# Two projections split or stacked, row sums moved, and transpositions joined, in a fused recurrent and FP4 feed-forward kernel on TensorE

## What is computed

```python
s = attn(xn)                       # causal convolution, min-GRU, feed-forward with gelu
h = silu(fp4(xn) @ fp4(w_gate).T) * (fp4(xn) @ fp4(w_up).T)     # 704 hidden columns
g = silu(fp4(h) @ fp4(w_down).T)
out = x + s * g
```

## Time and profile before

| | |
|---|---|
| median of 3 runs | 1085.59 us (1084.41 to 1086.84) |
| the profiled execution | 1085.26 us |
| its span, first to last instruction | 1083.5 us |
| mean granted clock of TensorE in it | 0.997 of 2.4 GHz |
| busy share of TensorE, VectorE, ScalarE, GpSimd | 98%, 86%, 56%, 14% |
| from chunk to chunk in the middle | 63.98 us |

### The profile page before, as it was taken

One profiled execution on the slowest core, in us unless ns is written; L12 is line 12 of the kernel. 1 busy time (PEld: TensorE's weight loads), 2 busy tenths in 40 slices (PEclk: granted clock), 3 DMA queues, 4 the chain that ended last, 5 costly groups with the idle time before them and its releaser, 6 DMA issues. The chain is left out here.

```text
span 1083.5 us, 18319 instructions
## 1 busy us (share of the span) xinstructions
PE 1061.8 (98%) x6954; PEld 967.9 (89%) x6954; DVE 934.5 (86%) x1720; ACT 607.3 (56%) x967; POOL 147.5 (14%) x123
## 2 busy tenths in 40 slices
PE   7899999999999999999999999999999999999998
PEld 6788989989898998989999898998989899898998
DVE  6978988989888898988889898898989889898895
ACT  5564464564746547474654747455574645647452
POOL 1230101112020110201111010111101011120010
PEclk9999999999999999999999999999999999999999
DMA  7000001010010101001010010101001010100110
GB/s 248 1 21 1 1 2 59 1 60 1 1 59 1 59 1 47 13 2 59 1 60 1 21 40 1 59 1 60 1 1 59 1 59 1 59 1 2 39 40 21
DMA packets 29365, 31.45 MB, mean 29 GB/s; under 512 B 1120, under 2 KB 28512, under 8 KB 29280
## 3 DMA queue, kind: packets, MB, share of 16 engines
q1 hardware_dynamic: 28448, 29.43, 8.7%
q10 hardware_dynamic: 832, 0.87, 0.2%
HBM read 21.90 MB, written 8.39 MB: 28 GB/s over the span
## 5 line engine op out<-in xcount | busy, mean ns | idle before, releaser
L990 PE MATMUL gu_ps<-gu_hi,xq_hi 128*128 128x352 f32 x512 | 168.3, 329 | 0.0
L990 PE MATMUL gu_ps<-gu_lo,xq_hi 128*128 128x352 f32 x512 | 165.9, 324 | 0.0
L990 PE MATMUL gu_ps<-gu_hi,xq_lo 128*128 128x352 f32 x512 | 165.7, 324 | 0.0
L990 PE MATMUL w_ps<-w_hi,act_hi 128*128 128x256 f32 x480 | 140.1, 292 | 0.0
L990 PE MATMUL w_ps<-w_hi,act_lo 128*128 128x256 f32 x480 | 135.1, 281 | 0.0
L990 PE MATMUL w_ps<-w_lo,act_hi 128*128 128x256 f32 x480 | 134.9, 281 | 0.0
L990 PE MATMUL w_ps<-dn_hi,hqt_hi 128*128 128x256 f32 x384 | 116.6, 304 | 2.0 <-DVE hqt_lo L519 2.0
L990 PE MATMUL w_ps<-dn_hi,hqt_lo 128*128 128x256 f32 x384 | 108.5, 283 | 0.0
L990 PE MATMUL w_ps<-dn_lo,hqt_hi 128*128 128x256 f32 x384 | 108.4, 282 | 0.0
L818 ACT ACTIVATE g<-w_ps 128x256 f32<-128x256 f32 x64 | 24.7, 385 | 147.7 <-PE w_ps L990 147.6
L496 DVE TENSOR_TENSOR hid<-sl,gu_ps 128x704 f32<-128x704 f32 x64 | 56.8, 887 | 58.8 <-PE gu_ps L990 58.2
(11 more groups left out here) (136 smaller groups left out, 2703.6 us busy)
## 6 DMA issues: line engine op xcount, KB each, us to landing
x_in<-x_dram SPq DMA_DIRECT2D x16, 512.0 KB, 5.8
x_res<-x_dram SPq DMA_DIRECT2D x16, 512.0 KB, 5.0
out_dram<-o SPq DMA_DIRECT2D x15, 512.0 KB, 3.5
act<-w_t_dram SPq DMA_DIRECT2D x1, 1024.0 KB, 11.3
w_f<-w_t_dram SPq DMA_DIRECT2D x1, 1024.0 KB, 13.8
w_f<-w_down_dram SPq DMA_DIRECT2D x1, 704.0 KB, 9.4
hid<-w_gate_dram SPq DMA_DIRECT2D x1, 640.0 KB, 5.9
hid<-w_up_dram SPq DMA_DIRECT2D x1, 640.0 KB, 9.3
```

The source lines that it names most:

```text
L990: done = M.matmul(psum, l, r, start=first and i == 0, stop=last and i == len(terms) - 1)
```

## The change

Seven edits:

1. **Split pointwise.** `pw` and `y` get high and low parts (`pw_hi`, `pw_lo`, `y_hi`, `y_lo`), so that the product runs as three fp32r matmuls for each block. `y_hi` is cast on ScalarE (`front_y_high`), `y_lo` is subtracted on VectorE (`front_y_low`).
2. **Stacked half slice.** `hq` holds the last 64 hidden columns twice instead of zeros. `hidden_low` leaves the low part of the last slice in the upper half of `hqt_hi`'s slice, and `down` needs two matmuls for it instead of three.
3. **Moved sums.** The row sums (`front_stats`) of chunk c + 2 stand at the end of body c, the aggregates (`front_moments`) after `hidden_values(c - 1, 2)`. SP's load of x_in stands ahead of the store.
4. **act_lo** runs as four and four instead of five and three. `output_sum` isn't changed.
5. **Joined transpositions.** `ff2_open` is a function of its own, called for tiles 0 and 1 together. `front_xc` and the opening of tile 2 stand between ff2 of tile 3 and ff2 of tile 2. `pointwise` transposes both banks of xn first.
6. VectorE's and ScalarE's queues in the front change order: the taps ahead of the FP4 values, `output` of tile 1 ahead of `scaled_low`.
7. **The start.** Low parts of ff1's and ff2's weights move from GpSimd to VectorE (`ff_low`), the weight pieces 3 to 5 move behind, between parts of ff1, and the counts of `keep_busy` change.

```diff
@@ SP
             with sp.Fori(0, B - 3) as i:
+                load(i + 3)
                 store(i)
-                load(i + 3)
@@ GpSimd, first()
-            def low_weights(j):
+            def gru_low():
...
                 rms_scale(0)
-                pool.wait_ge(xslo_ready, KD)
-                low_weights(1)
                 rms_scale(1)
-                pool.wait_ge(xslo_ready, 2 * KD)
-                low_weights(2)
@@ VectorE
+            def fp4_hidden_values(dst, rounded):
+                n, last = NBI * FP4_BLOCK, NFULL * P // FP4_BLOCK
+                fp4_values(dst[:, 0:n], NBI, rounded)
+                return V.scalar_tensor_tensor(blocks(dst[:, n:KI * P], NBI - last),
+                                              blocks(q_m[:, NFULL * P:n].bitcast(BF16), NBI - last),
+                                              1.0 / UNIT, spread(q_scale[:, last:NBI], NBI - last),
+                                              ALU.mult, ALU.mult)
+            def front_y_low(c):
+                for k in range(KD):
+                    dve.wait_ge(yhi_ready, KD * c + k + 1)
+                    V.tensor_tensor(y_lo[:, k, :], y[:, k, :], y_hi[:, k, :].bitcast(F32),
+                                    ALU.subtract).then_inc(ylo_ready, 1)
@@ VectorE, hidden_low
-                V.tensor_tensor(hqt_lo[:], hqt_ps, hqt_hi[:].bitcast(F32), ALU.subtract).then_inc(hqtlo_ready, 1)
+                V.tensor_tensor(hqt_lo[:], hqt_ps[:, 0:NFULL, :], hqt_hi[:, 0:NFULL, :].bitcast(F32), ALU.subtract)
+                twin = hqt_hi[LAST:P, NFULL, :]
+                V.tensor_tensor(twin, hqt_ps[LAST:P, NFULL, :], twin.bitcast(F32),
+                                ALU.subtract).then_inc(hqtlo_ready, 1)
@@ VectorE, first(), in part
+                ff_low(1)
                 recurrence(0, 0)
                 recurrence(0, 1)
-                scales = weight_scales(4)
+                scales = weight_scales(3)
...
                 scaled_low(1)
+                for p in (4, 5):
+                    weight_values(p, weight_round(p, weight_ratios(p, weight_scales(p))))
+                ff_low(2)
@@ VectorE, body
                 hidden_values(c - 1, 1, fp4_round(NBI, carried["ratios"]))
-                gelus_low(c - 1, range(5))
+                gelus_low(c - 1, range(4))
                 hidden(c, 0)
...
                 clamp_sums(c * 2, w_ps[:, 0, :])
                 hidden_values(c - 1, 2, fp4_round(NBI, ratios))
-                gelus_low(c - 1, range(5, KF))
+                if front and c > 1:
+                    front_moments(carried["stats"])
+                gelus_low(c - 1, range(4, KF))
                 hidden(c, 2)
...
-                if front:
-                    front_moments(c + 1)
+                if front and c == 1:
+                    front_moments(front_stats(c + 1))
                 recurrence(c, 0)
...
+                output(c - 1, 1, w_ps[:, 1, :])
                 scaled_low(c * 2 + 1)
-                output(c - 1, 1, w_ps[:, 1, :])
...
                 if front:
-                    front_fp4_values(c + 1, front_fp4_ratios(c + 1))
+                    ratios = front_fp4_ratios(c + 1)
                     front_taps(c + 1)
+                    front_fp4_values(c + 1, fp4_round(T * NBD, ratios))
+                    front_y_low(c + 1)
                     carried["ratios"] = fp4_ratios(hid[:, 1, :], NBI, hidden_scales(c, 1))
                     hidden_low(c, 0)
                     front_fp4_low(c + 1)
+                    if c + 2 < B:
+                        carried["stats"] = front_stats(c + 2)
@@ ScalarE, body
-                for j in range(KF // 2):
+                gelus(c, (0,))
+                if front:
+                    front_y(c + 1)
+                gelus_high(c, (0,))
+                for j in range(1, KF // 2):
                     gelus(c, (j,))
                     gelus_high(c, (j,))
                 if front:
-                    front_y(c + 1)
-                    gelus(c, range(KF // 2, KF))
+                    gelus(c, range(KF // 2, KF - 2))
+                    front_y_high(c + 1)
+                    gelus(c, range(KF - 2, KF))
@@ TensorE, pointwise
+                pe.wait_ge(y_ready, KD * (c + 1))
                 for e in range(KD):
-                    pe.wait_ge(y_ready, KD * (c + 1))
                     for t in range(T):
                         M.matmul(w_ps[:, e, t * P:(t + 1) * P], xn[:, t, e * P:(e + 1) * P], ident[:],
                                  is_transpose=True, start=t == 0, stop=False)
+                pe.wait_ge(yhi_ready, KD * (c + 1))
+                pe.wait_ge(ylo_ready, KD * (c + 1))
+                for e in range(KD):
                     for k in range(KD):
-                        last = product(w_ps[:, e, :], pw[:, k, e * P:(e + 1) * P], y[:, k, :], False, k == KD - 1)
+                        last = product(w_ps[:, e, :], (pw_hi[:, k, e * P:(e + 1) * P], pw_lo[:, k, e * P:(e + 1) * P]),
+                                       (y_hi[:, k, :], y_lo[:, k, :]), False, k == KD - 1)
@@ TensorE, down
-                for k in range(KI):
-                    last = product(bank[:, 0:D], (hqt_hi[:, k, :], hqt_lo[:, k, :]),
-                                   (dn_hi[:, k, :], dn_lo[:, k, :]), k == 0, k == KI - 1)
-                last.then_inc(dn_done, 1)
+                for k in range(NFULL):
+                    product(bank[:, 0:D], (hqt_hi[:, k, :], hqt_lo[:, k, :]), (dn_hi[:, k, :], dn_lo[:, k, :]),
+                            k == 0, False)
+                M.matmul(bank[:, 0:D], hqt_hi[:, NFULL, :], dn_lo[:, NFULL, :], start=False, stop=False)
+                M.matmul(bank[:, 0:D], hqt_hi[:, NFULL, :], dn_hi[:, NFULL, :], start=False,
+                         stop=True).then_inc(dn_done, 1)
@@ TensorE, body
-                ff2(c - 1, 0, w_ps[:, 0, :], (ss_ready, 2 * c + 1))
-                ff2(c - 1, 1, w_ps[:, 1, :], (xs_ready, KD * (2 * c + 1)))
+                ff2_open(c - 1, 0, w_ps[:, 0, :], (ss_ready, 2 * c + 1))
+                ff2_open(c - 1, 1, w_ps[:, 1, :], (xs_ready, KD * (2 * c + 1)))
+                ff2(c - 1, 0, w_ps[:, 0, :])
+                ff2(c - 1, 1, w_ps[:, 1, :])
...
-                ff2(c - 1, 3, w_ps[:, 3, :], (hqtlo_ready, T * c))
-                ff2(c - 1, 2, w_ps[:, 2, :], (g_ready, T * c))
-                ff1(c, range(KF // 2))
+                ff2_open(c - 1, 3, w_ps[:, 3, :], (hqtlo_ready, T * c))
+                ff2(c - 1, 3, w_ps[:, 3, :])
                 if front:
                     pe.wait_ge(sg_ready, T * c - 2)
                     front_xc(c + 1)
+                ff2_open(c - 1, 2, w_ps[:, 2, :], (g_ready, T * c))
+                ff2(c - 1, 2, w_ps[:, 2, :])
+                ff1(c, range(KF // 2))
```

More of the change, by code:

```diff
@@ L101, in mixed_recurrent_kernel @@
         b1c = cols[:, KD * 9:KD * 9 + KF]
-        pw = sb("pw", [P, KD, D])
+        pw_hi = sb("pw_hi", [P, KD, D], F32R)
+        pw_lo = sb("pw_lo", [P, KD, D], F32R)
         gru_hi = sb("gru_hi", [P, KD, 2 * D], F32R)
@@ L137, in mixed_recurrent_kernel @@
         xs_lo = sb("xs_lo", [P, KD, L], F32R)
-        keep = sb("keep", [P, KD, L])
+        keep, y_hi = shared_home(("keep", [P, KD, L], F32), ("y_hi", [P, KD, L], F32R))
         take = xs
-        cand = sb("cand", [P, KD, L])
+        cand, y_lo = shared_home(("cand", [P, KD, L], F32), ("y_lo", [P, KD, L], F32R))
         y = cand
@@ L151, in mixed_recurrent_kernel @@
         hqt_hi = sb("hqt_hi", [P, KI, P], F32R)
-        hqt_lo = sb("hqt_lo", [P, KI, P], F32R)
+        hqt_lo = sb("hqt_lo", [P, NFULL, P], F32R)
         q_amax = sb("q_amax", [P, 64])
@@ L204, in mixed_recurrent_kernel @@
         y_ready = sem("y_ready")
+        yhi_ready = sem("yhi_ready")
+        ylo_ready = sem("ylo_ready")
+        pwhi_ready = sem("pwhi_ready")
+        pwlo_ready = sem("pwlo_ready")
         xqhi_ready = sem("xqhi_ready")
@@ L439, in front_moments @@
                     last = V.bn_stats(stats[:, t, :], x_in[:, t, :])
-                s = steps.mark(last)
+                return steps.mark(last)
+            def front_moments(s):
                 dve.wait_ge(dve_step, s)
@@ L757, in front_y, with front_y_high @@
                                  scale=dww[:, k, 2:3]).then_inc(y0_ready, 1)
+            def front_y_high(c):
+                for k in range(KD):
+                    act.wait_ge(y_ready, KD * c + k + 1)
+                    act.wait_ge(pw_done, KD * c)
+                    act.wait_ge(x2_ready, KD * c)
+                    A.copy(y_hi[:, k, :], y[:, k, :]).then_inc(yhi_ready, 1)
             def front_xq(c):
@@ L883, in first @@
                 act.wait_ge(ld_const, 32)
-                A.activation(minus_ident[:], ident[:], ACT.Copy, scale=-1.0).then_inc(minus_ready, 1)
+                A.activation(minus_ident, ident[:], ACT.Copy, scale=-1.0).then_inc(minus_ready, 1)
                 act.wait_ge(small_ready, 1)
+                act.wait_ge(ld_pw, 16)
```

(9 more changed lines are left out.)

189 lines of the change are left out of this document (104 added, 85 removed).

## The result

The changed kernel takes **1144.2 us** (median of 4 runs, 1143.7 to 1145.2) against 1085.0 us (1084.2 to 1086.8) before, a ratio of 1.054 (95% interval 1.0526 to 1.0563). It is slower by 59 us. The prediction was 1135.5 us, 1107 to 1159.

The account below looks back on a forecast made before the run. TensorE's issue rate was taken as the bound. 1083.5 - 15.2 (savings) + 53.9 (wait) - 0.6 (last chunk) + 17.5 (clock) - 5 (start) - 0.4 (tail) = 1133.7 us of span, forecast 1135.5, range 1107 to 1159.

Parts of the forecast that it names:

- Part 5: At the first scale, inv_rms queued behind GpSimd's output sum makes TensorE wait 3.85 us, 14 times: +53.9 us.
- The lock: VectorE and GpSimd exclude each other: o waits for the sixth act_lo, adding 0.47 us to TensorE's wait for inv_rms.
- The clock: Behind each inv_rms wait TensorE runs 3.4 us at half clock, costing 1.25 us a time: +17.5 us.
- The savings: TensorE's work per chunk without a new wait: -0.65 - 0.48 + 0.12 = -1.01 us, over 15 chunks -15.2 us.
- Part 1: Pointwise product: eight fp32 records become 12 fp32r products, -0.65 us a chunk on TensorE, +1.21 on VectorE.
- Part 3: Joined transpositions: fewer borders between transpositions and products give back 0, not over 0.02 us a border either way.
- Part 2: Stacked half slice in down: 17 matmuls instead of 18, -0.48 us a chunk on TensorE, some +0.8 on VectorE.
- the part that is eaten: At the second scale, one of down's four savings turns into longer waiting for GpSimd: +0.12 us a chunk.
- VectorE would hold 58 of 63.0 us, no bound: VectorE's added work per chunk, 56.0 + 2.0 us, was claimed not to limit the chunk.
- `hqt_lo` 0.4 us ahead of down: VectorE's hqt_lo was to be ready 0.4 us before down needs it, so a new wait of 0.
- my first rival: No new wait at inv_rms because o doesn't come between; only savings stay, 1064.7 us; chance 0.09.
- Part 4: Moved row sums and aggregates free VectorE ahead of the recurrence, where TensorE doesn't wait for it: 0.

Follow-up runs that it names:

- e5: The changed kernel with GpSimd's output sum queued behind the next chunk's first power, ahead of its layernorm, threshold still five; 1113.1 us, ratio 1.0256.
- e1: The changed kernel with the threshold of GpSimd's output sum lowered from the fifth act_lo to the fourth; 1089.3 us, ratio 1.0035.
- e4: The changed kernel with the threshold of GpSimd's output sum raised from the fifth act_lo to the eighth; 1165.0 us, ratio 1.0736.
- e2: The kernel before with one edit alone, act_lo as four and four instead of five and three; 1149.0 us, ratio 1.0592.
- e7: The changed kernel with 16 idle TensorE matmuls ahead of the first scale's transposition in chunks 2 to 15; 1121.7 us, ratio 1.0327.
- e9: e6 with the pointwise product in plain fp32 again; 1090.4 us, ratio 1.0045.
- e8: e6 with the joined transpositions taken apart into their old groups; 1083.9 us, ratio 0.9984.
- e12: e11 with the stacked half slice undone, six plain slices and 18 products in down; 1071.4 us, ratio 0.9869.
- e11: e6 with hqt_lo and the low part of xs on VectorE ahead of the fourth hidden rows' scales; 1069.6 us, ratio 0.9855.
- e10: e6 with the layernorm's sums and aggregates back ahead of the recurrence; 1087.3 us, ratio 1.0017.
- e3: The changed kernel with 30 idle TensorE matmuls ahead of the inv_rms transposition in every body, which overshoot the wait; 1165.4 us, ratio 1.0745.
- e6: The changed kernel with the threshold at four and VectorE's scales of hidden tile 1 ahead of y_lo; 1081.8 us, ratio 0.9962.

## Why the prediction was right, and where its steps were not

**Part 5, the wait, was right step by step.** I had the fifth `act_lo` 1.12 us ahead of the moment at which TensorE wants inv_rms (565.60 and 566.72). In the trace the fifth starts at 657.47, and TensorE, which waits 3.84 us counted from start to start up to 662.43, would have gone on at 658.59: 1.12. From its end to o 0.13, from inv_rms to TensorE 0.05, both as taken. The wait of 3.85 was 3.84. Experiment 5 of GpSimd's queue (e5) and the threshold (e1, e4) show from both sides that it is the order in the queue and the threshold together; e2 shows that the split alone does it.

**The lock had the right size by the wrong picture, which is luck.** The 0.47 were to come from o starting when the sixth `act_lo` is done. But o is printed from 658.29, while the sixth runs to 658.76 at its usual length. Instead o is 0.26 longer than in the earlier trace rows and inv_rms 0.23, together 0.49, and it is the seventh `act_lo` that waits for o's end (2.8 us instead of 0.69), as in the earlier trace rows. Whether o's printed start is its real one the trace doesn't tell.

**The clock was taken too low.** I took 1.25 us a wait between 0 and 1.7, and it was 1.6 (e7). The term is 22.4, not 17.5. The slow stretch, 663.10 to 666.50, starts 0.7 us behind the wait's end, and in thirteen of the fourteen nothing of it falls into the wait, which was my reason for less than 1.7; where 1.2 us of it do, at the first, it is 6.8 us long and costs 1.0 more. What I had in mind does happen in e2: at equal waits of 2.87 us its periods are 68.26 to 68.31 us where 0.66 us or more of the stretch lie in the wait, and 68.50 to 68.58 where none does. By the rule of the Trainium skill that I quoted, "TensorE: Matmul & The Clock Gate", HAM oscillation, the term would have been 23.8. The trace agrees with it: the clock fell at each of the 14 waits.

**The savings were right, in sum and by part, on one condition.** Part 1: -0.65 predicted, 0.65 in e9. Part 3: 0, and 0 in e8. Part 2: -0.36 with the part that is eaten, -0.26 in e12; the mis-sized term is VectorE's work, which I had priced at 0.8 us of its queue and which is 1.7, since the second subtraction takes a slot of 0.33 us and not 0.15 and the first is hardly shorter (0.83 to 0.87). Its lateness costs the 0.1. The sum, 62.97, is e11's 63.02. The condition is the step that failed: **"VectorE would hold 58 of 63.0 us, no bound", and `hqt_lo` 0.4 us ahead of down, "I take 0".** VectorE does hold 58.8 of 63.0, but `y_lo`'s wait for ScalarE (up to 1.7 us) and the new small operations push its queue late just where `hqt_lo` is wanted. In the changed kernel this is hidden: VectorE catches up while TensorE waits for inv_rms. With that wait gone, e1 loses 1.4 us a chunk against e11, and TensorE waits for `hqt_lo` twice in it (up to 0.47 and 0.84). So my first rival, no new wait at 1064.7, had a price that would not have come true: 1089 with the change's own order, 1069.6 with two calls moved.

**Part 4** was taken as 0 and is worth 0.31 us a chunk in e10, as a balance of two waits. In the kernel before TensorE didn't wait ahead of the recurrence; in e10, with 2.6 us a chunk more on VectorE than there (58.66 and 56.03), it does.

**The ends.** The start gave 3.7 and not 5, within my bounds. The last part lost 1.4 instead of gaining 1.4. TensorE waits in it for `act_lo` longer than before, and the clock falls, which it didn't before. In e1 the same wait of 2.12 us has no fall behind it, and the last part is 61.5 us: the fall costs 1.6. TensorE's wait in the tail, before and after, and the stretches behind them:

```profile
1060.03 0.41 PE L1109 MATMUL gu_ps<-ident,x2b 128*128 128x128 f32 x2 [1.74 <-issue]
1060.00:1063.40 3.40, 3.37 (x29) 3.40 (x30) 3.30 (x7) 0.81 (x2) 0.00 (x0) 1.00 0.02 5
```

```profile
1119.09 0.36 PE L1061 MATMUL gu_ps<-w_hi,act_hi 128*128 128x256 f32 x1 [2.12 <-DVE act_lo L530]
1120.20:1123.60 3.40, 3.40 (x19) 3.40 (x18) 3.24 (x7) 0.00 (x0) 0.00 (x0) 0.54 0.00 0
```

Clock 4.9, the first period 1.9, the start 1.3 and the last part 2.8 make 10.9 us; the chunks' other work is 0.07 us shorter than 62.97, which gives 1.0 back. That accounts for the 9.7 us between the predicted span of 1133.7 and 1143.4 to within 0.2. Of the first period's 1.9 us, 1.0 is its long slow stretch and 0.9 is a later start of the sums of squares behind its first ff2 (in e7 too). There TensorE waits 0.68 us for the place at which it waits in every chunk of e10, and chunk 1 is the one that still has the sums of rows ahead of the recurrence.

## What to carry to other kernels

A semaphore's threshold into another engine's count is a place in that engine's order: whoever moves or splits the counted operations must ask again what stands behind the waiting instruction in its in-order queue. Price a wait of TensorE with the slow clock behind it, and when the wait has been removed, look at what it had hidden. A share of 93% on a helper engine is no bound and no all-clear either: read, for each of its results, the slot at which it stands and the moment at which it is wanted, and put operations with slack behind those with none.

## What the hardware showed

- Of TensorE's idle times, those of 1.52 us and of 1.57 and 1.74 us (tails of e12 and of the kernel before) were not followed by a slow clock, nor were the 14 of 1.55 us in e5. Those of 1.96 and 1.97 us in the start of the kernel before (the first is in the earlier trace rows) were. Those of 2.12 to 2.15 us, all at the same place in the tail, were in six profiles (the changed kernel, e4, e7, e8, e10, e11) and were not in five (e1, e3, e5, e6, e9): at that length the same wait goes either way. All 14 of 2.9 to 3.2 us in e2, of 3.1 to 3.7 in the changed kernel and of 4.2 to 4.7 in e4 met one.
- At these 42 waits the stretch at 0.50 was 3.4 us long 34 times and 6.8 us long eight times (once in e2, once in the changed kernel, six times in e4). The 34 began between 0.7 us before the end of the wait and 1.1 us after it, the eight between 0.9 and 1.3 us before it.
- A large tensor operation of GpSimd (128 x 1024) with `act_lo` in flight on VectorE lets one more `act_lo` through and holds the next till its own end, 2.2 us, alike in the changed kernel, e2 and e5 (the four take 4.64, 4.65 and 4.69 us). The starts are as printed. In e1 it held a 44-element operation (q_wide) just so, but not hid and the reduction ahead of that, 0.88 us each as ever, which lay wholly or mostly beside it.
- GpSimd's power of 4 elements for each partition takes 1.01 us with VectorE idle and 1.46 beside `act_lo`: the tiny operation is lengthened by 0.45 us, and o, of 128 x 1024 elements, by 0.33 (2.34 and 2.67).
- An idle fp32 matmul of 128 columns is two records of 0.112 us.
